# A top-k selection that asks three candidates a round, and a first block turned tile by tile

## The reference, cut to what matters

```python
n_tok = b * s                     # 32 * 512 = 16384
k = n_tok // E                    # 2048 rows an expert
logits = xf @ Wr + br
Sm = jax.nn.softmax(logits, axis=-1)
G_t, idx_t = jax.lax.top_k(Sm.T, k)          # each expert takes its k best rows
tokens = xf[idx]
mid = jax.nn.silu(jnp.einsum('keh,ehf->kef', tokens, Wu) + bu)   # h 512 -> f 1365
out = jnp.einsum('kef,efh->keh', mid, W_down) + b_down           # f 1365 -> 512
y = jnp.zeros_like(xf).at[idx].add(G[..., None] * out)
x = x + jnp.tanh(g_ffn[0]) * y
```

## Time and profile before

| what | value |
|---|---|
| median of 3 runs | 3332.16 us (3329.63 to 3335.16) |
| profiled execution, device time | 3335.54 us |
| its span | 3333.8 us |
| PE matmul busy | 3059.0 us (92%) |
| PE weight loads busy | 2407.0 us (72%) |
| DVE busy | 1941.6 us (58%) |
| ACT busy | 1277.3 us (38%) |
| POOL busy | 1039.7 us (31%) |

### The profile page before, as it was taken

One profiled execution on the slowest core, in us unless ns is written; L12 is line 12 of the kernel. 1 busy time (PEld: TensorE's weight loads), 2 busy tenths in 40 slices (PEclk: granted clock), 3 DMA queues, 4 the chain that ended last, 5 costly groups with the idle time before them and its releaser, 6 DMA issues.

```text
span 3333.8 us, 60389 instructions
## 1 busy us (share of the span) xinstructions
PE 3059.0 (92%) x23964; PEld 2407.0 (72%) x24092; DVE 1941.6 (58%) x5529; ACT 1277.3 (38%) x2860; POOL 1039.7 (31%) x949
## 2 busy tenths in 40 slices
PE   4888898888988828999999999999999999999998
PEld 3677777776777616777777777778778778778886
DVE  4788887888888765544545544544553554553332
ACT  3678877788887731111112112113112112211210
POOL 3456656566565631111211111121111112112111
PEclk9899999999999958999999999999999999999999
DMA  3143333433334241213213222223123223212211
GB/s 106 53 140 116 129 116 115 141 116 124 121 119 138 78 122 42 46 28 79 42 36 102 34 46 73 34 47 100 32 34 71 48 35 91 57 31 41 68 31 25
DMA packets 140065, 250.67 MB, mean 75 GB/s; under 512 B 31456, under 2 KB 31456, under 8 KB 139784
## 3 DMA queue, kind: packets, MB, share of 16 engines
q1 hardware_dynamic: 106104, 170.80, 15.3%
q0 software_dynamic: 28672, 67.65, 11.5%
q10 hardware_dynamic: 5008, 8.36, 0.8%
HBM read 137.23 MB, written 101.19 MB: 72 GB/s over the span
## 4 chain that ended last, share of the span: by engine, by line
PE 55%; DVE 5%; DMA 2%; issue 1%; ACT 0%; POOL 0%; DVEq 0%; ACTq 0%; POOLq 0%
PE UP L1434 27%; PE DN L1460 26%; PE TT L1413 2%; DMA w_raw<-in_L_ffn_W_down 1%; DVE c_early L1243 1%; DVE c_within L1185 1%; DVE c_hit L1174 0%; DVE c_cand L1205 0%; PE c_bank L1160 0%; DVE c_begun L1184 0%; ACT z L1386 0%; DVE xT_lo L1471 0%; DVE down_lo L1072 0%; DVE mid_lo L1491 0%; DVE y L1511 0%
## 5 line engine op out<-in xcount | busy, mean ns | idle before, releaser
L1360 POOL DMA_INDIRECT out_x<-y,slots x128 | 201.2, 1572 | 1687.3 <-DVE y L1513 1687.3
L1460 PE MATMUL DN<-down_hi,mid_hi 128*128 128x512 f32 x1408 | 588.5, 418 | 0.0
L1386 ACT ACTIVATE z<-UP,bup 128x512 f32<-128x512 f32 (+1 forms) x352 | 240.9, 686 | 881.6 <-PE UP L1434 858.2
L1434 PE MATMUL UP<-xT_hi,up_hi 128*128 128x512 f32 (+1 forms) x1408 | 554.6, 394 | 2.8 <-DVE xT_lo L1471 1.5
L1434 PE MATMUL UP<-xT_hi,up_lo 128*128 128x512 f32 (+1 forms) x1408 | 555.9, 395 | 0.0
L1434 PE MATMUL UP<-xT_lo,up_hi 128*128 128x512 f32 (+1 forms) x1408 | 552.5, 392 | 0.0
L1460 PE MATMUL DN<-down_hi,mid_lo 128*128 128x512 f32 x1280 | 505.5, 395 | 0.0
L1460 PE MATMUL DN<-down_lo,mid_hi 128*128 128x512 f32 x1280 | 504.8, 394 | 0.0
L1489 DVE CAST mid_hi<-z 128x512 fp32r<-128x512 f32 (+1 forms) x352 | 151.1, 429 | 498.2 <-ACT z L1386 486.9
L1369 ACT ACTIVATE xT_hi<-TT 128x512 fp32r<-128x512 f32 x128 | 76.3, 596 | 731.6 <-PE TT L1413 731.6
L1434 PEld LDWEIGHTS UP<-xT_hi,up_hi 128*128 128x128 f32 (+1 forms) x1408 | 260.4, 185 | 71.5 <-ACT z L1386 6.4
(11 more groups left out here) (229 smaller groups left out, 5115.8 us busy)
## 6 DMA issues: line engine op xcount, KB each, us to landing
xs<-in_x SPq DMA_DIRECT2D x32, 1024.0 KB, 8.1
kraw<-in_ctx SPq DMA_DIRECT2D x32, 1024.0 KB, 6.7
out_x<-xs SPq DMA_DIRECT2D x32, 1024.0 KB, 5.4
rows_scratch<-xfb SPq DMA_DIRECT2D x32, 1024.0 KB, 4.3
w_raw<-in_L_ffn_W_down SPq DMA_DIRECT2D x40, 512.0 KB, 4.6
w_raw<-in_L_ffn_W_up SPq DMA_DIRECT2D x16, 682.5 KB, 4.1
mid_hi<-mid_hi ACTq DMA_DIRECT2D x32, 86.0 KB
mid_lo<-mid_hi ACTq DMA_DIRECT2D x32, 84.0 KB
```

The source lines that it names most:

```text
L1360: pool.indirect_dma_start(out_rows, bass.IndirectOffsetOnAxis(ap=slots[:, m:m + 1], axis=0), y[:, t, :], None, compute_op=ALU.add).then_in ...
L1386: act.activation(z[0:r, k % 2, :], UP[k % 3][0:r, :], ACT.Silu, bias=bup[0:r, e // 2, f:f + 1]).then_inc(s["z"], 1)
L1434: mm = pe.matmul(UP[k % 3][0:r, :], weights.up[wa][:, c, f * P:f * P + r], xT[xa][:, c, :], start=first, stop=(c == CH - 1 and wa == 1))
L1460: mm = pe.matmul(DN[m % 2][:, :], lhs, rhs, start=first, stop=(f == FCH - 1 and lhs is parts[-1][0]))
```

## The change

1. **Rounds.** The bit steps go two bits a round. `reach` forms three candidates at once (`c_cand`, 128x3: the known part plus 1, 2 and 3 times the lower bit's value), counts three times (three `c_hit`), and PE's product has four columns. The answer is one `scalar_tensor_tensor` that clamps all four columns and sums them. A `memset` writes the caps behind the counts. 7 upper and 8 lower rounds take the place of 14 and 16.
2. **Groups.** A `rows` step now does four columns of 128 slots, one block's; four steps in place of six. The 129th column of `places` goes: the last value's column carries the partition's first position. `listed(n)` is n + 1, so the first gather needs one group, not two. The list of steps is 22 long.
3. **Placement.** `SELECT_AT` is (2, 7): two steps a down tile, fifteen matmuls apart. The 18 steps up to `base` take nine tiles; the `rows` steps stand in the tenth (two), eleventh and twelfth.
4. **The first block.** Each of the four gathered tiles has its own semaphore. PE turns the first block by tiles, each as it lands, into four banks (the two `TT` and the two `DN`), and the first up product starts with chunk 0 while the others are being split. DVE's `gate(0)` stands behind the four `turn_lo`.
5. **The seam.** SP no longer waits for the stores at attention's end. POOL waits for `rows` and `probs` ahead of `gather(0)`, and for the stores of x behind it.
6. POOL makes two more constants ahead of the others, and PE and DVE wait for five of them, not seven and three.

```diff
@@ attention, SP's end
-                for n in range(XBUF):
-                    sp.wait_ge(s_xst[n], 16 * len(range(n, NB, XBUF)))
-                sp.wait_ge(s_rows, 16 * NB)
-                sp.wait_ge(s_probs, 16 * NB)
@@ Select.__init__
-        self.groups = [list(range(a, min(a + 3, self.KC))) for a in range(0, self.KC, 3)]
-        self.steps = [("turn", 0)] + [("upper", k) for k in range(self.TOP_BIT - self.LOWER, -1, -1)] \
-            + [("lower", k) for k in range(self.LOWER - 1, -1, -1)] + [("ties", 0), ("base", 0)] \
+        self.groups = [list(range(a, a + TILES)) for a in range(0, self.KC, TILES)]
+        self.steps = [("turn", 0)] + [("upper", k) for k in range(self.TOP_BIT - self.LOWER - 1, -1, -2)] \
+            + [("lower", k) for k in range(self.LOWER - 2, -1, -2)] + [("ties", 0), ("base", 0)] \
             + [("rows", g) for g in range(len(self.groups))]
@@ Select.product
         elif kind in ("upper", "lower"):
-            mm = pe.matmul(pc, self.huge[:, :], self.count[:, :], start=True, stop=True)
+            mm = pe.matmul(bank[:, 508:512], self.huge[:, :], self.count[:, :], start=True, stop=True)
...
-                mm = pe.matmul(bank[:, j * (P + 1):(j + 1) * (P + 1)], self.within[g % 2][:, j * P:(j + 1) * P], self.places[:, :],
+                mm = pe.matmul(bank[:, j * P:(j + 1) * P], self.within[g % 2][:, j * P:(j + 1) * P], self.places[:, :],
                                start=True, stop=True)
@@ Select.reach
-        dve.tensor_scalar(self.hit[:, :], values, cand[:, :], self.less[:, :], ALU.is_ge, ALU.add, accum_out=self.count[:, :])\
-            .then_inc(self.asked, 1)
-        half = float(1 << (bit - 1)) if bit else 0.0
-        dve.tensor_scalar(self.ends[:, 0:1], cand[:, :], -half if bit else -1.0, None, ALU.add)
-        self.step(dve.tensor_scalar(self.ends[:, 1:2], cand[:, :], half, None, ALU.add))
+        self.step(dve.tensor_scalar(self.cand[:, :], self.threes[:, :], float(1 << bit), known[:, 0:1], ALU.mult, ALU.add))
+        for j in range(3):
+            ins = dve.tensor_scalar(self.hit[:, j, :], values, self.cand[:, j:j + 1], self.less[:, :], ALU.is_ge, ALU.add,
+                                    accum_out=self.count[:, j + 1:j + 2])
+        ins.then_inc(self.asked, 1)
+        dve.memset(known[:, 1:4], float(1 << bit)).then_inc(self.own, 1)
+        self.step.line.n += 1
@@ Select.decide
-            step(dve.tensor_scalar(new[:, :], pc, self.ends[:, 0:1], self.ends[:, 1:2], ALU.max, ALU.min))
+            dve.wait_ge(self.own, step.line.n)
+            step(dve.scalar_tensor_tensor(out=self.gained[:, :], in0=bank[:, 508:512], scalar=0.0, in1=old[:, :], op0=ALU.max, op1=ALU.min,
+                                          accum_out=new[:, 0:1]))
@@ Select.listed
-        e, last = n * TILES // self.KC, (n * TILES + TILES - 1) % self.KC
-        return len(self.groups) * e + last // 3 + 1
+        return n + 1
@@ experts
+        def turned(n, c):
+
+            return (T + DN)[c] if n == 0 else T[c % 2]
...
-        SELECT_AT = (2, 4, 6, 8)
+        SELECT_AT = (2, 7)
+        light = len(select.steps) - BPE
 
         def next_steps(n, t):
 
-            e, first = n // BPE + 1, ((n % BPE) * 4 + t) * len(SELECT_AT)
-            return {f: first + j for j, f in enumerate(SELECT_AT) if e < NEXP and first + j < len(select.steps)}
+            e, at = n // BPE + 1, ((n % BPE) * 4 + t) * 2
+            if e == NEXP:
+                return {}
+            if at < light:
+                return {f: at + j for j, f in enumerate(SELECT_AT) if at + j < light}
+            rows = {light: (0, 1), light + 2: (2,), light + 4: (3,)}.get(at, ())
+            return {f: light + g for f, g in zip(SELECT_AT, rows)}
@@ experts, POOL
+                pool.wait_ge(stored["rows"], 16 * (NTOK // SEQ))
+                pool.wait_ge(stored["probs"], 16 * (NTOK // SEQ))
                 gather(0)
+                for k in range(XBUF):
+                    pool.wait_ge(stored["x"][k], 16 * len(range(k, NTOK // SEQ, XBUF)))
@@ experts, PE
-                for c in range(CH):
-                    turn(0, c)
+                for t in range(4):
+                    pe.wait_ge(s_rows[t], 16)
+                    for c in range(CH):
+                        mm = pe.transpose(turned(0, c)[:, t * P:(t + 1) * P], xg[:, t, c * P:(c + 1) * P], ident[:, :])
+                        if t == 3:
+                            mm.then_inc(s["tfull"], 1)
...
+                            if n == 0 and at == 0:
+                                pe.wait_ge(s["tlo"], c + 1)
@@ experts, DVE
-                gate(0)
                 for c in range(CH):
                     turn_lo(0, c)
+                gate(0)
```

More of the change, by code:

```diff
@@ L1140, in constants @@
         step(pool.memset(self.less[0:1, :], 0.5 - float(self.K) / P))
+        step(pool.memset(self.count[:, 0:1], 1.0))
+        step(pool.iota(self.threes[:, :], pattern=[[1, 3]], base=1, channel_multiplier=0, allow_small_or_imprecise_dtypes=True))
         step(pool.memset(self.ahead32[:, :], 1.0))
@@ L1197, in decide @@
         if kind == "turn":
-            step(dve.memset(self.cand[0][:, :], float(1 << (self.TOP_BIT - self.LOWER))))
+            step(dve.memset(self.gain[0][:, :], 0.0))
             step(dve.tensor_copy(self.V[:, :], bank[:, 0:P]))
             if e == 0:
-                dve.wait_ge(self.made, 3)
-            self.reach(dve, upper, self.cand[0], self.TOP_BIT - self.LOWER)
+                dve.wait_ge(self.made, 5)
+            self.reach(dve, upper, self.gain[0], self.steps[i + 1][1])
         elif kind in ("upper", "lower"):
-            old, new = self.cand[(i - 1) % 2], self.cand[i % 2]
@@ L1208, in decide @@
             elif kind == "upper":
-                dve.tensor_copy(self.low[:, :], new[:, :])
-                step(dve.scalar_tensor_tensor(out=self.key[:, :], in0=upper, scalar=new[:, :], in1=lower, op0=ALU.is_equal, op1=ALU.mult))
-                step(dve.tensor_scalar(self.beyond[:, :], upper, new[:, :], float((1 << self.LOWER) - 1), ALU.is_gt, ALU.mult))
-                step(dve.memset(new[:, :], float(1 << (self.LOWER - 1))))
+                dve.tensor_copy(self.low[:, :], new[:, 0:1])
@@ L1213, in decide @@
+                step(dve.scalar_tensor_tensor(out=self.key[:, :], in0=upper, scalar=new[:, 0:1], in1=lower, op0=ALU.is_equal, op1=ALU.mult))
+                step(dve.tensor_scalar(self.beyond[:, :], upper, new[:, 0:1], float((1 << self.LOWER) - 1), ALU.is_gt, ALU.mult))
+                step(dve.memset(new[:, :], 0.0))
                 step(dve.tensor_tensor(self.key[:, :], self.key[:, :], self.beyond[:, :], ALU.add))
-                self.reach(dve, self.key[:, :], new, self.LOWER - 1)
+                self.reach(dve, self.key[:, :], new, self.LOWER - 2)
@@ L1283, in experts @@
         T = [ctx.enter_context(nc.psum_tensor(f"TT{n}", [P, BLK], FP32)) for n in range(2)]
-        s = {n: sem(n) for n in "bup rows up z hi mid dn yp y tfull thi tlo gs dve laid".split()}
+        s = {n: sem(n) for n in "bup up z hi mid dn yp y tfull thi tlo gs dve laid".split()}
+        s_rows = [sem(f"rows{n}") for n in range(4)]
         s_sc = [sem(f"sc{n}") for n in range(4)]
```

67 lines of the change are left out of this document (37 added, 30 removed).

## The result

| | before | changed |
|---|---|---|
| median | 3333.01 us (3329.63 to 3335.16, 4 runs) | 3287.68 us (3280.61 to 3293.39, 4 runs) |
| profiled execution, device time | 3335.54 us | 3293.39 us |
| its span | 3333.8 us | 3291.4 us |

What follows compares the result with a forecast made beforehand. PE was taken to set the time in the experts' half, and an unhidden chain at the seam. Savings of 42 + 2.2 + 4.1 + 1.5 = 49.8 us gave 3285.7 profiled, 3282 us against the median, range 3274 to 3299.

Steps and rivals of the forecast that it cites:

- Part 1, the steps in the down tiles: Selection steps inside the experts' down tiles: cost falls from 9.5 to 3.45 us an expert, 42 us saved for seven.
- the share of waits: Of the old steps' 9.5 us an expert, 3.9 were put down to PE waiting for DVE.
- Part 2, the search of expert 0: From the seam to the first gather: fifteen rounds of 1.90 us replace thirty of 1.09; 2.2 us saved in all.
- the three candidates are a small op with an immediate and a pointer; ... with its step 0.20: In each round of expert 0's search, forming the candidates was priced at 0.20 us of the round's 1.90.
- The search is held as I say: Expert 0's key and its sum wait for POOL's subtractions, the sum ending at 1225.3: 2.2 us saved, 3282 us, chance 0.50.
- its two rivals: Expert 0's search half free of POOL's holds (4.9 us saved, 3280, chance 0.22) or wholly free (8.3, 3276, chance 0.10).
- Part 3, the first block: From the last gathered tile's landing to the first up product: 6.1 us becomes about 1.95, 4.1 us saved.
- Part 4, the seam: Between attention's end and the experts' first load: 1.5 us saved (0 to 1.8); POOL's new waits are for stores issued long before.
- the named rivals: Freer search (3280, 0.22; 3276, 0.10), rows steps wait (3298, 0.12), late light answers (3310 to 3331, 0.03), slower (3339, 0.03).
- a slower kernel: In the down tiles DVE's answers come later than PE's next question: about 3339 us, chance 0.03, elsewhere 0.02.

Runs made afterwards that it cites:

- before_apart: The kernel before, all 39 steps kept, with three steps a down tile, nine matmuls apart: 3303.56 us, ratio 0.9933.
- turn_back: The changed kernel with the first block's sixteen transposes again chunk by chunk in two banks, `gate(0)` ahead of the four `turn_lo`: 3290.01 us, ratio 0.9891.

## Why the prediction was right, and where it was not

**Part 1, the steps in the down tiles: right, in size and in cause.** 42 us were forecast; 41.2 came in the profiled pair from the first up product on, 42.4 when the clock's gain and the stall are set apart. Block lengths, the cost of a light and of a row step, and the share of waits each came out within a few hundredths to a tenth. No wait at a selection product is left in the changed kernel's list.

**Part 2, the search of expert 0: wrong.** The step that failed is "the three candidates are a small op with an immediate and a pointer; ... with its step 0.20". Its free length is right (0.24, the round 1.83). But in the very part that follows the holds of POOL, I asked only of operations with two inputs whether they could be held. The candidates' operation stands in every round, POOL is at work for more than half of that time, and so it was caught nine times in fifteen, for 12.5 us. "The search is held as I say" and its two rivals were all about one key and its sum; the key's sum in fact slipped through. In place of -2.2 it was +4.9 in this execution (0.64 of it the delay ahead of the gather, see Part 4), and from +1.2 to +4.9 over six, since it depends on which rounds meet which subtractions. Against the 49.60 us of the old search in `before_apart` all of these are 1.1 lower, the least of them +0.1: no draw was a gain, but the size is a draw on both sides. With the candidates one column wide, the same reasoning gives 46.3 and the runs 45.2 and 46.5.

**Part 3, the first block: right** (4.1 forecast, 4.2), **but a term was missing.** I priced the first up products "at its lower clock there" and took that as given, though the change itself puts work on PE just ahead of them. It gave 2.4 us more in the profiled pair, and less in the executions in which the clock rose late.

**Part 4, the seam: right** (1.5 forecast, 1.47), **with a cost left out.** POOL's new waits were judged only by whether the stores would be done. They were, and still cost 0.64 us by their place.

**The sum.** 49.8 us were forecast and the profiled pair shows 42.4. Of the 7.4 between them 7.1 are the search. The rest nearly cancels: the stall in expert 1 (3.6) against the clock (2.4), 0.4 of Part 1 and 0.4 by which attention ended earlier. The medians are 45.3 apart, since the profiled execution was the slowest of the changed kernel's four, with the dearest of the six searches and the stall. None of the named rivals happened. (The chance of a slower kernel stands in the prediction once as 0.03 and once as 0.02; nothing hangs on it.)

## What to carry to other kernels

When a search or a scalar loop on DVE runs beside streaming work on POOL, go through every DVE operation of the loop and not only the large ones: a three-column operation of 0.23 us cost more than all the arithmetic that the new rounds saved. A question between two engines inside a stream of matmuls should stand further from the last one than the whole answer takes; that distance is read from the round of a stretch where nothing else runs, and waits of 0.3 us hide in the overlap of matmul records. And put waits that are surely met where the engine is idle anyway, not ahead of the wait that decides.

## What the runs showed of the chip that I had not expected

- A `tensor_scalar` on 128x3 f32 in SBUF was held by POOL's running subtraction, for 3.07 us in `turn_back` and up to 2.92 in the changed kernel's profile, and for 1.35 by POOL's `iota`, which only writes; with one input on 128x1 it was never held in 360 executions (155 ns at most) beside the same subtractions. Two inputs were held at one column too (`c_past`, 1.99 us instead of 0.16). A `tensor_scalar` of 128x128 from uint16 to f32 (`c_beyond`, 0.29 us) took 2.25 in the changed kernel. The counts, `tensor_scalar` of 128x128 that also write a sum, were never held (0.41 us at most).
- Two waits already met, directly ahead of a third, put 0.64 us more between the event and POOL's DMA (0.94 instead of 0.30).
- The same work on PE ahead of the first up product did not fix the moment at which the granted clock rose: between 2.2 us before that product and 3.5 us behind it, in nine executions of the same order. And after a wait of PE of 2.1 us in the middle of expert 1 the clock was 0.50 for 3.4 us.
- A late down-weight load (11.14 us) cost 3.6 us in one execution's first block of expert 1, 2.1 of wait and the rest of clock; in another the same load took 7.20 us and cost nothing like it. What delays it was not tried.
